# Where the keys of the last cross attention are formed: routing, list and gather of a mixture-of-experts layer

## The reference

```python
x = x + _L0_attn_ref(_layernorm(x), ...)
x = x + _L0_xattn_ref(_layernorm(x), ctx_1024, ctx_1024, mask, ...)
x = x + _L0_ffn_ref(_layernorm(x), ...)      # router: sigmoid scores, 4 of 8 groups, 8 of 64 experts, plus a shared expert
x = x + _L1_attn_ref(_layernorm(x), ...)
x = x + _L1_xattn_ref(_layernorm(x), fside, fside, mask, ctx_1024, ctx_1024, ...)
x = x + _L1_ffn_ref(_layernorm(x), ...)      # router: 2 of 8 experts

def _L1_xattn_ref(queries, keys, values, attention_mask, key_grid, value_grid, ...):
    k = keys @ Wk.T + bk                     # 16 heads of 64: 1024 wide
    gk = key_grid @ Wgk.T + bgk
    k_new = concatenate([k, gk], axis=1)     # 256 keys and 256 grid keys a sequence
    v = values @ Wv.T + bv
    gv = key_grid @ Wgv.T + bgv
    v_new = concatenate([v, gv], axis=1)
    ...                                      # scaled, masked softmax attention, projection
```

## Time and profile before

| | |
|---|---|
| median of 3 runs | 4519.63 us (4510.0 to 4520.34) |
| profiled execution | 4516.43 us |
| its span, first to last instruction | 4514.9 us |
| mean granted TensorE clock | 0.921 of full speed |
| busy PE / DVE / ACT / POOL | 3916.9 / 2713.2 / 1961.2 / 2259.9 us |
| mean DMA rate | 119 GB/s |

### The profile page before, as it was taken

How to read it: one execution, slowest core, us unless ns; L and a number is a source line. 1 busy time by engine, 2 the same in 40 slices (tenths; PEclk the granted TensorE clock), 3 DMA queues, 4 the chain that set the end, 5 groups by cost and what they waited for, 6 DMA issues and landing times. The chain is left out here.

```text
span 4514.9 us, 100102 instructions
## 1 busy us (share of the span) xinstructions
PE 3916.9 (87%) x33128; PEld 3174.9 (70%) x33128; DVE 2713.2 (60%) x7291; ACT 1961.2 (43%) x4070; POOL 2259.9 (50%) x2482
## 2 busy tenths in 40 slices
PE   6998799964889999688969996999999998499991
PEld 5777577643578888677757774767677776399991
DVE  4775566568944443355546663777777775855553
ACT  2554355533223323222224443666666664155550
POOL 2332322123056666565645542676667674256665
PEclk8999899966999999899979997999999998599996
DMA  1000000001279999777710003434443441265653
GB/s 53 1 0 1 30 12 9 3 29 44 94 236 299 300 299 302 236 258 256 257 49 1 0 1 99 107 85 104 104 104 97 96 106 38 88 228 211 226 194 119
DMA packets 294493, 539.05 MB, mean 119 GB/s; under 512 B 37760, under 2 KB 136449, under 8 KB 283265
## 3 DMA queue, kind: packets, MB, share of 16 engines
q1 hardware_dynamic: 153600, 338.81, 22.3%
q0 software_dynamic: 107264, 136.38, 12.1%
q10 hardware_dynamic: 33408, 60.83, 3.5%
HBM read 378.60 MB, written 140.51 MB: 115 GB/s over the span
## 5 line engine op out<-in xcount | busy, mean ns | idle before, releaser
L2049 POOL DMA_INDIRECT L_ffn_xin<-zs,L_ffn_listed x464 | 501.0, 1080 | 298.6 <-issue 165.0
L562 POOL TENSOR_TENSOR L_xattn_p<-L_xattn_p,L_xattn_rsum 128x1024 f32<-128x1024 f32 x256 | 484.2, 1891 | 222.9 <-DVE L_xattn_rsum L664 219.5
L2409 POOL DMA_INDIRECT L_ffn_back<-ys,L_ffn_slots x320 | 310.9, 971 | 203.8 <-DVE x_res L2426 85.3
L2081 PE MATMUL L_ffn_bank<-L_ffn_xT,L_ffn_w 128*128 128x256 f32 x1536 | 367.4, 383 | 4.9 <-ACT L_ffn_xT L2148 3.1
L599 DVE TENSOR_REDUCE L_xattn_negmax<-L_xattn_scores 128x2 f32<-128x1024 f32 x256 | 310.4, 1212 | 80.4 <-PE L_xattn_scores L771 80.4
L1305 ACT ACTIVATE L_attn_pT<-L_attn_bank 128x384 f32<-128x384 f32 x512 | 223.3, 488 | 296.5 <-PE L_attn_bank L1411 157.1
L698 ACT ACTIVATE L_xattn_p<-L_xattn_scores,L_xattn_negmax 128x512 f32<-128x512 f32 x512 | 346.4, 687 | 5.3 <-DVE L_xattn_negmax L599 4.5
L2148 ACT ACTIVATE L_ffn_xT<-L_ffn_bank 128x512 f32<-128x512 f32 (+1 forms) x232 | 137.8, 594 | 409.2 <-DVE L_ffn_yo L2307 193.9
L2081 PEld LDWEIGHTS L_ffn_bank<-L_ffn_xT,L_ffn_w 128*128 128x128 f32 x1536 | 279.0, 192 | 38.7 <-issue 5.1
L783 PE MATMUL L_xattn_turned<-ident,L_xattn_p 128*128 128x128 f32 x2048 | 270.0, 275 | 27.7 <-POOL L_xattn_p L562 27.7
L2300 DVE TENSOR_TENSOR L_ffn_hid<-L_ffn_sg,L_ffn_bank 128x256 f32<-128x256 f32 x192 | 80.9, 422 | 328.5 <-issue 189.9
(11 more groups left out here) (385 smaller groups left out, 11435.0 us busy)
## 6 DMA issues: line engine op xcount, KB each, us to landing
L_ffn_w<-in_L_ffn_w SPq DMA_DIRECT2D x80, 1024.0 KB
L_ffn_w<-in_L_ffn_w SPq DMA_DIRECT2D x192, 384.0 KB
ys<-L_ffn_yo ACTq DMA_DIRECT2D x232, 256.0 KB
kv<-kv_v_row SPq DMA_DIRECT2D x128, 256.0 KB
L_xattn_mask<-in_L_xattn_mask POOLq DMA_DIRECT2D x256, 128.0 KB, 2.5
L_xattn_k_raw<-kv SPq DMA_DIRECT2D x128, 256.0 KB, 2.6
L_xattn_v<-kv SPq DMA_DIRECT2D x16, 2048.0 KB, 9.5
kv<-kv_k_row SPq DMA_DIRECT2D x96, 256.0 KB
```

What stands on the lines that cost most here:

```text
L562: pool.tensor_tensor(p[:, s % 4, :, :], p[:, s % 4, :, :], rsum[:, s % 2, :, None].to_broadcast([P, 2, c.keys]), ALU.mult).then_inc(n_read ...
L2049: pool.indirect_dma_start(xin[j % U][:, t, :], None, zs, bass.IndirectOffsetOnAxis(ap=listed[:, 2 * j + t:2 * j + t + 1], axis=0)).then_in ...
L2081: return pe.matmul(out, a[0], b[0], start=first, stop=last)
L2409: pool.indirect_dma_start(back[:, i % NG, :], None, ys, bass.IndirectOffsetOnAxis(ap=slots[:, tile, k:k + 1], axis=0)).then_inc(b_in[i % N ...
```

## The change

The keys of sequences 0 to 2 (24 units) are formed in the routing of `L0_ffn`, those of sequences 3 to 7 (40 units) in its list, and those of sequences 8 to 15 (64 units) in its gather, where sequences with keys and sequences with values alone now alternate. In the routing, steps 2 to 13 take two units each, one before and one after the ranks. To have what they need there, the key weights and the sources of two sequences are loaded at the routing's start into buffers of their own, ahead of the stores of `z`, and split in its steps 0 and 1; the sources of the third and fourth sequence are split in steps 6 and 10, those of four more in the list. The loads of the first experts are issued at the start of the list. The routing of both feed-forward parts is written out step by step in place of the loops, and so the last two steps have no statistics or normalising.

```diff
-    LISTED = 8 * QUADS
+    KEYED = (0, 2)
+    ROUTED = 24
+    LISTED = 8 * (B - QUADS * len(KEYED)) - ROUTED
+    FIRST_STEP, PER_STEP, BEFORE_RANKS = 2, 2, 1
...
+    def units_of(self, step):
+        first = (step - self.FIRST_STEP) * self.PER_STEP
+        units = [n for n in range(first, first + self.PER_STEP) if 0 <= n < self.ROUTED]
+        return units[0:self.BEFORE_RANKS], units[self.BEFORE_RANKS:]
...
+    def rounded_after(self, n):
+        return n // 8 + 1 if n % 8 == 1 and 1 <= n // 8 and 8 * (n // 8 + 1) < self.ROUTED + self.LISTED else None
...
             @block.sync
...
-                with sp.Fori(0, B // 2, 1) as pair:
...
+                if keys:
+                    keys.load_key_weights(sp)
...
+                store_z(0)
+                store_z(1)
+                for b in range(B):
+                    before, after = keys.units_of(b) if keys else ([], [])
+                    for unit in before:
+                        keys.store_unit(sp, unit)
+                    if b + 2 < B:
+                        store_z(b + 2)
+                    for unit in after:
+                        keys.store_unit(sp, unit)
...
-                with pool.Fori(0, B, 1) as b:
-                    deviation(b + 2)
+                for b in range(B):
+                    if b + 2 < B:
+                        deviation(b + 2)
                     if moe0:
                         shared_form(b)
                         shared_add(b)
+                    if keys and b < 2:
+                        keys.split_key_weight(pool, b)
+                        keys.split_unit_sources(pool, b)
...
-                with dve.Fori(0, B // 2, 1) as pair:
-                    for u in range(2):
-                        b = pair * 2 + u
+                for b in range(B):
+                    if b + 2 < B:
                         statistics(b + 2)
-                        choose(b, sc2[u])
-                        normalise(b + 2, u)
-                        number(b)
+                    choose(b, sc2[b % 2])
+                    if b + 2 < B:
+                        normalise(b + 2, b % 2)
+                    number(b)
...
                     if moe0:
                         shared_gate(b)
-                    if not last:
-                        scores(b + 1, 1 - u)
+                    if b + 1 < B:
+                        scores(b + 1, 1 - b % 2)
+                    before, after = keys.units_of(b) if keys else ([], [])
+                    for unit in before + after:
+                        keys.take_unit(act, unit)
                     if moe0:
                         shared_take(b)
...
-                with pe.Fori(0, B // 2 - 1, 1) as pair:
...
+                for b in range(B):
+                    if b + 1 < B:
+                        logits(b + 1, 1 - b % 2)
+                    before, after = keys.units_of(b) if keys else ([], [])
+                    for unit in before:
+                        keys.make_unit(pe, unit)
                     ranks(b)
+                    for unit in after:
+                        keys.make_unit(pe, unit)
                     shared_down(b)
...
-        keys_at = {24 + 7 * unit: unit for unit in range(keys.LISTED)} if keys else {}
+        keys_at = {12 + 6 * unit: keys.ROUTED + unit for unit in range(keys.LISTED)} if keys else {}
...
+                load_first()
                 if keys:
-                    keys.list_sync(sp, load_first)
-                else:
-                    load_first()
+                    keys.list_sync(sp)
...
         unit_at, passed = {}, 0
+        measure = [20 if keys and unit // 8 % 4 in keys.KEYED else 12 for unit in range(8 * B)]
         for unit in range(8 * B):
-            unit_at[16 + passed * (len(order) - 16) // (8 * B // 4 * (3 * 20 + 12))] = unit
-            passed += 12 if unit // 8 % 4 == 3 else 20
+            unit_at[16 + passed * (len(order) - 16) // sum(measure)] = unit
+            passed += measure[unit]
```

220 lines of the change are left out of this document (112 added, 108 removed).

## The result

The changed kernel takes 4556.3 us (median of 4 runs, 4552.9 to 4570.5), the kernel before on the same chip 4519.1 (4 runs). The ratio is 1.0089, with a 95% interval of 1.0069 to 1.0109: the change makes the kernel 0.9% slower, where 4456 us had been predicted. The profiled execution has a span of 4553.8 us against 4514.9 before.

What follows compares the result with a forecast made beforehand. Bounds by stretch: DVE in list and routings, PE in the gather with POOL nearly level. Gather -50, layer 0's routing 0, preparation -8.4, list +7, layer 1's routing -12: -63.4, about 4456 us; range 4430 to 4490.

Steps and rivals of the forecast that it cites:

- The change touches stretches of about 1,000 us out of 4,515: Whole kernel: only layer 0's routing, list and gather and layer 1's routing were priced; other stretches were given no change.
- Rival 5: Written-out routings: PE's crawl behind "issue" recurs in straight code, 18 us lost per patch, 4528 us or more; chance 0.04.
- The real pace ... 1.70 us each with all stalls: Gather: 188 units in 320 us, so 32 key units fewer save 54.5 us; -50 was taken.
- Rival 3: Gather becomes POOL's: some 50 of its 79 us of waits stay, so -30 there, 4476 in all; chance 0.13.
- GpSimd's floor of 1.25 us: Gather: 256 indirect DMAs at 1.25 us of POOL each make 320 us, so at most 81 us can go.
- the chain ... hidden but for jitter, +3: Layer 0's routing: two key units bring the PE and ACT chain to 10.6 us, within about 12 free; +3 us.
- Rival 2: Layer 0's routing set by PE and ACT: each step grows 2 to 3.5 us, +25 to +42 in all; chance 0.15.
- the chain's other matmuls likewise: Layer 0's routing: at full clock L1855 and the chain's other matmuls get shorter, some 2 us in all per step.
- writing out layer 0's loop: Layer 0's routing: branch and register waits go, -8.5 us, and statistics and normalising over padding go, -3.4 us.
- the splits of steps 0 and 1: Layer 0's routing: 14.2 us of POOL splitting two key weights and two source pairs beside DVE's chain cost +8.5 us.
- The -3 for L1774: Layer 0's routing: POOL's shared-expert addition no longer falls on this DVE line, 1.07 us saved in three steps.
- rival 4: Both routings: writing out gives nothing because the "issue" waits are drains, not the loop; 4473 us; chance 0.06.

Runs made afterwards that it cites:

- head_where_after_has_it: Kernel before plus 56 semaphore increments on PE, putting the layer 1 cross attention loop's head 13 instructions ahead of a page's end; ratio 1.0107.
- written_out_alone: Kernel before with both layers' routing written out step by step, plus 228 increments on PE keeping the later loop's head at its old place; ratio 1.0033.
- half_of_the_picks_gathered: Changed kernel with 24 increments and every second expert-output gather left out, DVE adding each gathered one twice; gather 281.2 us, ratio 0.9672.

## Why the prediction was wrong

Of 100 us between 4456 and 4556, 39 are in a stretch that the prediction left out, 36 in the gather, 18 in layer 0's routing; the other 7 are within what unchanged stretches differ by.

1. **The failed step that made it slower and not the same: "The change touches stretches of about 1,000 us out of 4,515".** It touches every stretch, since it moves the code behind it. The rival of that kind (5, slower) looked for the cost in the straight code, by the earlier trace rows; what the runs showed is a loop, a layer on and untouched, whose head came to stand 13 instructions ahead of a page's end. head_where_after_has_it brings 1034.7 of the 1038.1 us without the change. The Trainium skill (Runtime: NRT & Kernel Launch, "Instruction fetch mechanics") says that a taken branch whose target is outside the fetched pages stalls. The prediction used this for the routings' loops and not for the loops that stay; the trace agrees with it here too, with 3.3 to 4.4 us at each return of this loop. Rival 5's own ground, the crawl of the earlier trace rows, is not one of straight code: its 2.1 us are three times 0.70, a pitch that SyncE shows in the gather too, in its loops as well; the routings written out have hardly any of it (in layer 0's, 0.7 us at most on PE and 2.1 on SyncE), and with half of the gathers left out the same straight code of the gather has none on PE.
2. **The failed term of the gather: "The real pace ... 1.70 us each with all stalls", -50; it measured -14.** The pace per unit was taken for a price, and it is a quotient: 320 us over the units that happened to pass. At 256 gathers the stretch hardly follows PE's work: 1.62 us a gather before, 1.56 after, 1.53 with PE's key work nearly gone. (This is a quotient too, and no price: with 128 gathers it is 2.20.) The -14 are this pair of traces; nine traces of the changed gather have 405.5 us on average and five of the old one 413.4, 8 us less. Rival 3 had the right engine and stopped at -30, because it charged GpSimd's floor of 1.25 us and its waits as if they could be packed; the runs show them uneven in time, GpSimd held when DVE waits for PE and PE held when DVE waits for its picks, so that 75 us off PE gave 12 to 14. The tests in the text say the same: GpSimd from its first to its last gather was to take 350 us and took 389.3 (400.7 before), and its waits, to be under 40 us, are 64.8.
3. **The failed term of the routing: "the chain ... hidden but for jitter, +3"; it measured +16 to +18**, with the two splits of steps 6 and 10 in it, for which +3 more had been taken. Rival 2 was right in mechanism and had +25 to +42. The clock was not the low one throughout (0.81 in all, 0.84 in the steps with units), but where it counts: the units ran fast, and the logits and shared product behind the wait for ACT slow. The prediction's "the chain's other matmuls likewise" get the upper level was wrong just there.
4. **Mis-sized:** writing out layer 0's loop, -3.4 to -5.6 for -11.9; the splits of steps 0 and 1 +7 for +8.5 (the Trainium skill's rule of the exclusive lock, SBUF — State Buffer, "Who interferes with whom", would by itself have given +14: of GpSimd's 14.2 us some 9 were felt in the two steps beside the splits, and 7 over the stretch). The four operations of the preparation are 10.0 - 1.7 = 8.3, not 8.4. The -3 for L1774 can be read from the traces: DVE spends 10.5 us in it in the 16 steps before (7 of them long), 5.5 in the changed kernel (1 long), so -5.0, but 14.9 in written_out_alone (13 long). This +4.4 is most of what writing out alone fell short by, for DVE's waits on "issue" ahead of statistics and gate did go, from 9.8 us to 0.4. The +3 for later pairs wasn't tried by itself; with the units behind the shared product, units and later pairs together are about 1 us (178.6 and 177.7 us for 177.4).
5. **Right:** the preparation (-7.8 for -8.4), the list (+4.5 for +7), layer 1's routing (-10.3 for -12). DVE's waits on "issue" there are gone, as in layer 0, with which rival 4 falls.

What stays open: the first blocks of layer 1 are 4 us longer in every kernel with that routing written out; why gathers hold PE up inside its units (its products start late, by single instructions, with all 256 gathers and not under the denser transfers of half_of_the_picks_gathered) was not taken apart, the load of small transfers and the order of waits were cut together; and that a fetch lengthens a drain rests on the two going together, in the traces at hand and at the two places tried for it: how is not seen.

## What to carry to other kernels

A change that adds or removes instructions moves every loop behind it on that engine; where a loop's return shows a pause on "issue", compare that pause before and after, and try the kernel with the loop's head moved before you judge the change. A quotient such as "us per unit" in a stretch prices nothing until an experiment has taken the units or their partner away; the partner (here the gathers) may be the count that matters. Work that is to be hidden belongs where its engine has nothing urgent behind it: the same 24 units, two a step, cost 16 to 18 us ahead of a chain and about 1 us behind it. Padding that moves code has a price of its own, to be read from the trace and taken off before a ratio is judged.
